# Giving three of 32 channel-block statistics to ScalarE in a GroupNorm, BatchNorm and binary 3x3 convolution kernel

## The chip, the cores and the metric

The kernel runs on one core of one Trainium2 chip. Its time is device time in microseconds (us), the median of three runs. The core's engines run side by side: TensorE (PE) multiplies matrices, VectorE (DVE) and ScalarE (ACT) work elementwise and reduce along rows, GpSimd (POOL) does elementwise work and issues transfers, SyncE (SP) issues transfers. They meet only at semaphores. SBUF is the on-chip memory with 128 partitions, PSUM holds matmul results.

## The reference

The input x is 16 images of 256 channels, 56 x 56 pixels, float32.

```python
g = GroupNorm(x)                 # 32 groups of 8 channels per image: mean and variance
mean, var = over (image, h, w) of g, per channel
xn = (g - mean) * rsqrt(var + 1e-4) * gamma + beta
t  = where(xn > 0, 1, -1)
xc = clip(xn, -1, 1)
y  = conv3x3(t, conv_w) + conv_b                 # 256 -> 256 channels
b  = (conv3x3(sum_c(xc * t), ones) + beta_b) / (conv3x3(sum_c |t|, ones) + beta_b)
out = x + y * b
```

The convolution of an image can't start until the scale and offset of each channel are known, and these need the mean and the variance of every channel of all 16 images. So the kernel reads all of x once for the statistics, and again for the convolution.

## The kernel before, in words

Channels lie on the partitions: 256 channels are two halves of 128. A *block* is one channel half of one image, 128 x 3136 float32, 1568 KB. There are 32 blocks.

**Statistics.** SP issues the load of each block in order (`stat_load`, L186). Four buffers of one block each take turns: the two halves of `y` and the two halves of `xb`, which the convolution uses later for other data. Load k waits until VectorE has read block k - 4 (L190), then goes out on SP's queue, which is in order: a load that waits holds up all behind it. The two weight loads (L202) go out after the first two blocks. For each block VectorE runs `statistics(k)` (L657): it waits for the load, takes seven `bn_stats` of 448 columns (L662), and after the second of them combines the seven results of the block before with one `bn_aggr` (L654) into that block's mean and variance in `mv`. The last `bn_stats` counts `stats_read` up, which frees the buffer. Between blocks 7 and 8, and between 11 and 12, VectorE does small work on the weights' scale (L682 to L699). The last two blocks, 30 and 31, are the two channel halves of image 0; they are loaded as halves of rows, 812 KB each, four loads in all (L205 to L208), in the layout in which the convolution reads them, and take eight `bn_stats` of 392 columns (L673). In the meantime GpSimd and ScalarE prepare the weights (L303 to L325, L351 to L374). ScalarE's last weight step is L374; then it waits for the statistics.

**Coefficients.** When `aggr_done` says that all 32 are there, PE averages the means and variances over the groups of eight channels by three small matmuls (L543 to L548), ScalarE takes square roots (L378, L381), and VectorE computes scale and offset per image and channel into `AB` (L724 to L753); `coef_ready` then lets all engines go on.

**Convolution.** For each image and each of four pieces g (channel half, row half) VectorE and ScalarE turn x into signs and into the transformed planes `V`, PE multiplies them with the transformed weights `U` (L570), ScalarE and VectorE take results out, and GpSimd's queue adds x and stores. A hardware loop goes over the images.

Of the kernel before, what the change touches and what calls it, by code (L numbers as in the profile page):

```python
# [9 lines left out]
ACT = mybir.ActivationFunctionType  # L10
AX = mybir.AxisListType

P = 128
NI, C, H, W = 16, 256, 56, 56
# [21 lines left out]
TERMS = tuple((ci, digits, dx) for ci in range(CT) for dx in (1, 0, 2) for digits in range(2))  # L36
PIECES = 7
PIECE = H * W // PIECES

LAST_PARTS = ((0, N // 2), (N // 2, N))  # L40


def conv_preact(nc, x, w_t, gamma, beta, conv_b, beta_b, consts, sum_rows, map_rows, out):
# [6 lines left out]
    with ExitStack() as ctx:  # L50
        def sb(name, shape, dt=F32):
            return ctx.enter_context(nc.sbuf_tensor(name, shape, dt))

        def sem(name):
            return ctx.enter_context(nc.semaphore(name))
# [29 lines left out]
        inv_8 = sb("inv_8", [P, CT])  # L85
        st = sb("st", [P, 2, CT, 8, 6])
        mark = sb("mark", [P, 2, CT])
        mv = sb("mv", [P, NI, CT, 2])
        AB = sb("AB", [P, NI, 2, CT])
        eps = sb("eps", [P, 2])  # L90
# [22 lines left out]
        s_in = [[sem(f"s_in{a}{c}") for c in range(CT)] for a in range(2)]  # L113
        y_out = [sem(f"y_out{g}") for g in range(G4)]
        last_out = [sem(f"last_out{k}") for k in range(2)]
        x_added = [sem(f"x_added{g}") for g in range(G4)]
        stats_read, aggr_done = sem("stats_read"), sem("aggr_done")
        w_abs, wall, wrow, wscale = sem("w_abs"), sem("wall"), sem("wrow"), sem("wscale")
        w_pool, w_act, scale_ready = sem("w_pool"), sem("w_act"), sem("scale_ready")
        step, dev_ready, grp = sem("step"), sem("dev_ready"), sem("grp")  # L120
# [27 lines left out]
        def at_least(eng, s, value):  # L148

            if not (isinstance(value, int) and value <= 0):  # L150
                eng.wait_ge(s, value)

        def stat_image(k):

            pair, at = divmod(k, 4)
            return NI - 2 - 2 * pair + (at < 2), int(at < 2), at % 2

        def stat_buffer(a, c):

            if a:  # L160
                return y[:, 2 * c:2 * c + 2].rearrange("p g f -> p (g f)")
            return xb[:, c].rearrange("p h f -> p (h f)")[:, 0:H * W]

        def own_rows(g):

            first = W * (g // 2)
            return xb[:, g % 2, g // 2, first:first + HPX]
# [16 lines left out]
        @block.sync  # L184
        def _(sp):
            def stat_load(k):  # L186

                m, a, c = stat_image(k)
                if k >= 4:
                    sp.wait_ge(stats_read, k - 3)  # L190
                sp.dma_start(stat_buffer(a, c), x_rows[m, c]).then_inc(s_in[a][c], 16)

            def load_rows(src, g):

                h = g // 2
                first = (HR - 1) * W * h
                sp.dma_start(xb[:, g % 2, h], src[g % 2, :, first:first + XR * W]).then_inc(x_in[g], 16)

            stat_load(0)
            stat_load(1)  # L200
            for c in range(CT):
                sp.dma_start(wt[:, c], w_v[:, c].rearrange("p (a b o) -> p a b o", a=3, b=3)).then_inc(w_in[c], 16)  # L202
            for k in range(2, 2 * NI - 2):
                stat_load(k)
            for c in range(CT):  # L205
                sp.wait_ge(stats_read, 2 * NI - 5 + c)
                for g in (c, 2 + c):
                    load_rows(x_rows[0], g)  # L208

            def crow_load(m):  # L210

                sp.wait_ge(cs8_ready, m + 1)
                sp.dma_start(sum_rows[m, W:W + H * W].rearrange("(k f) -> k f", f=SQ), cs98[:, :])\
                  .then_inc(cs_stored, 16)
                sp.wait_ge(cs_stored, 16 * m + 16)
                at_least(sp, vsum_ready, m)
                sp.dma_start(crow[:, :, 1:W + 1], row_windows[m].rearrange("r (k w) -> r k w", w=W))\
                  .then_inc(crow_in, 16)

            def load(n, src, g):  # L220

                sp.wait_ge(u_ready, 4 * n + g + 4)
                sp.wait_ge(abs_done, 4 * n + g + 5)
                load_rows(src, g)

            def first_load(g):

                if g:
                    sp.wait_ge(u_ready, g)
                else:  # L230
                    sp.wait_ge(u0_ready, 1)
                sp.wait_ge(abs_done, g + 1)
                load_rows(x_rows[1], g)

            def map_load(n, h):

                if h:
                    at_least(sp, scaled, 4 * n)
                sp.dma_start(bmap[:, h, :],
                             map_rows[n:n + 1, h * HPX:(h + 1) * HPX].to_broadcast([P, HPX]))\  # L240
                  .then_inc(bmap_in[h], 16)

            def map_store(n):

                sp.wait_ge(bm_ready, n + 1)
                sp.dma_start(map_rows[n].rearrange("(r w) -> r w", w=W), bm[:, :]).then_inc(bm_stored, 16)
                sp.wait_ge(bm_stored, 16 * n + 16)

            def image(n, ahead=None):

                crow_load(n)
                if ahead is not None:
                    load(n, ahead, 0)
                map_store(n)
                map_load(n, 0)
                if ahead is not None:
                    load(n, ahead, 1)
                map_load(n, 1)
                if ahead is not None:
                    load(n, ahead, 2)  # L260
                if ahead is not None:
                    load(n, ahead, 3)

            for g in range(G4):
                first_load(g)
            load(0, x_rows[2], 0)
            load(0, x_rows[2], 1)
            sp.wait_ge(zeros_in, 16)
            crow_load(0)
            map_store(0)  # L270
            map_load(0, 0)
            map_load(0, 1)
            load(0, x_rows[2], 2)
            load(0, x_rows[2], 3)
            for n in range(1, NI - 2):
                image(n, x_rows[n + 2])
            image(NI - 2)
            image(NI - 1)

            for k, (lo, hi) in enumerate(LAST_PARTS):  # L280
                sp.wait_ge(last_added, k + 1)
                sp.dma_start(out_v[NI - 1, 1, 1][:, 4 * lo:4 * hi], y[:, 3, 4 * lo:4 * hi]).then_inc(last_out[k], 16)
            for g in range(G4):

                sp.wait_ge(y_out[g], 16 * (NI - (g == 3)))
            for k in range(2):
                sp.wait_ge(last_out[k], 16)
# [54 lines left out]
        def _(act):  # L342
# [31 lines left out]
                    nc.scalar.activation(U[:, ci, 0, k], src, ACT.Copy).then_inc(w_act, 1)  # L374


            act.wait_ge(grp, 3)
            nc.scalar.activation(tmp[:, 3, :], acc[:, 0, 0, 0:NI * CT], ACT.Sqrt, bias=eps[:, 0:1])\  # L378
              .then_inc(root_out, 1)
# [145 lines left out]
        def _(pe):  # L525
# [13 lines left out]

            pe.wait_ge(cst_in, 16)  # L540
            grouped = cst[:, C_GROUP:C_GROUP + P]
            pe.wait_ge(aggr_done, 2 * NI)
            nc.tensor.matmul(csum[:, 0:NI * CT], grouped, mv[:, :, :, 0].rearrange("p n c -> p (n c)"),  # L543
                             start=True, stop=True).then_inc(grp, 1)
            nc.tensor.matmul(acc[:, 0, 0, 0:NI * CT], grouped, mv[:, :, :, 1].rearrange("p n c -> p (n c)"),
# [86 lines left out]
        def _(dve):  # L632
# [16 lines left out]
            def aggregate(k):  # L649

                m, a, c = stat_image(k)
                dve.wait_ge(stats_read, k + 1)
                nc.vector.memset(mark[:, a, c:c + 1], 0.0)
                nc.vector.bn_aggr(mv[:, m, c, :], st[:, a, c] if k >= 2 * NI - 2 else st[:, a, c, 0:PIECES])\  # L654
                  .then_inc(aggr_done, 1)

            def statistics(k):  # L657

                m, a, c = stat_image(k)
                dve.wait_ge(s_in[a][c], 16 * (k // 4) + 16)  # L660
                for j in range(PIECES):
                    ins = nc.vector.bn_stats(st[:, a, c, j], stat_buffer(a, c)[:, j * PIECE:(j + 1) * PIECE])  # L662
                    if j == 1 and k:
                        aggregate(k - 1)
                ins.then_inc(stats_read, 1)

            def last_statistics(c):

                k = 2 * NI - 2 + c
                for h in range(2):  # L670
                    dve.wait_ge(x_in[2 * h + c], 16)
                    for j in range(4):
                        ins = nc.vector.bn_stats(st[:, 0, c, 4 * h + j], own_rows(2 * h + c)[:, j * N:(j + 1) * N])  # L673
                        if h == 0 and j == 1:
                            aggregate(k - 1)
                ins.then_inc(stats_read, 1)

            for k in range(8):
                statistics(k)
# [18 lines left out]
                                          ALU.mult, ALU.add))  # L698
            chain(nc.vector.reciprocal(rcount[:, :], rcount[:, :]))  # L699
            for k in range(12, 2 * NI - 2):  # L700
                statistics(k)
            for c in range(CT):
                last_statistics(c)
            aggregate(2 * NI - 1)

            mean = mv[:, :, :, 0].rearrange("p n c -> p (n c)")
# [14 lines left out]
                chain(nc.vector.scalar_tensor_tensor(out=s, in0=t, scalar=1.5, in1=s,  # L721
                                                     op0=ALU.add, op1=ALU.mult))

            dve.wait_ge(aggr_done, 2 * NI)  # L724
            dve.wait_ge(grp, 1)
            chain(nc.vector.tensor_tensor(d, mean, csum[:, 0:NI * CT], ALU.subtract))
            nc.vector.tensor_tensor(d2, d, d, ALU.mult).then_inc(dev_ready, 1)
# [283 lines left out]
```

## Time and profile before

| what | value |
|---|---|
| median of three runs | 937.71 us (937.62 to 938.79) |
| time of the profiled execution | 937.77 us |
| its span, from the first to the last instruction | 936.0 us |
| PE busy | 782.9 us, 84% |
| VectorE busy | 790.4 us, 84% |
| ScalarE busy | 581.3 us, 62% |
| GpSimd busy | 140.8 us, 15% |

The span and the time of the same execution are 1.77 us apart. Busy shares are averages over two very different stages. Of the 40 slices that the page cuts the span into (23.4 us each), the first six show PE nearly idle and VectorE full, and the slices behind them show PE full. The granted clock of PE in the same slices is 0.5 from the second to the sixth and 0.9 or more (of 2.4 GHz) behind them.

### The profile page before, as it was taken

The numbers are of one execution on the slowest core, as the hardware profiler recorded it, in microseconds if no ns is written. First come the engines' busy times: TensorE is split into PE (matmuls) and PEld (weight loads), VectorE is DVE, ScalarE is ACT, GpSimd is POOL, SyncE is SP. The second block draws the span as 40 slices with busy tenths as digits, with TensorE's granted clock in tenths as the row PEclk, the third lists the DMA queues.
The fourth block names the chain that finished last, engine by engine and source line by source line (L and its number), as shares of the span: only waits on it lengthen the run. The fifth ranks groups of instructions, "written<-read, shape, count | busy, mean of one in ns | idle before, by whom it ended". The sixth has DMA issues, their size and how long they took to land. (4 is left out here: it accounts for less than half of the span.)

```text
span 936.0 us, 12745 instructions
## 1 busy us (share of the span) xinstructions
PE 782.9 (84%) x4686; PEld 464.9 (50%) x4686; DVE 790.4 (84%) x1244; ACT 581.3 (62%) x469; POOL 140.8 (15%) x160
## 2 busy tenths in 40 slices
PE   2100003999999999999999999999999999999996
PEld 2100002555555555555555555555555555555553
DVE  4999998989888888888797979787878797879755
ACT  2043105968777777777777777776868686868310
POOL 0089300001111111101111111111111111101011
PEclk9755555999999999999999999999999999999998
DMA  9999972468888887888797969696969696958589
GB/s 360 429 408 377 411 323 70 142 182 259 252 249 231 243 238 220 265 213 275 192 296 174 314 161 318 163 310 165 308 171 297 174 297 185 293 157 215 131 214 268
DMA packets 43478, 232.79 MB, mean 249 GB/s; under 512 B 10560, under 2 KB 10688, under 8 KB 39360
## 3 DMA queue, kind: packets, MB, share of 16 engines
q0 software_dynamic: 18144, 101.16, 41.8%
q1 hardware_dynamic: 24544, 131.25, 38.7%
q10 hardware_dynamic: 768, 0.12, 0.1%
q8 instruction: 9, 0.15, 0.1%
q14 instruction: 13, 0.11, 0.0%
HBM read 180.73 MB, written 51.79 MB: 248 GB/s over the span
## 5 line engine op out<-in xcount | busy, mean ns | idle before, releaser
L570 PE MATMUL acc<-V,U 128*128 128x385 f16 (+1 forms) x4608 | 769.4, 331 | 11.8 <-DVE V L790 10.1
L570 PEld LDWEIGHTS acc<-V,U 128*128 128x128 f16 x4608 | 450.9, 98 | 325.8 <-issue 12.7
L442 ACT ACTIVATE sn<-acc,inv_s 128x784 f32<-128x784 f32 x128 | 116.9, 913 | 207.1 <-PE acc L570 201.2
L335 POOL DMA_DIRECT2D y<-x x63 | 53.9, 856 | 728.7 <-DVE y L877 715.2
L877 DVE SCALAR_TENSOR_TENSOR y<-y,vec,bmap 128x1568 f32<-128x1568 f32 (+1 forms) x65 | 117.7, 1810 | 0.2
L420 ACT ACTIVATE r<-xb,ab 128x1568 f32<-128x1568 f32 x64 | 106.6, 1690 | 6.0 <-ACT u L395 4.0
L395 ACT ACTIVATE u<-xb,ab 128x1624 f16<-128x1624 f32 x63 | 109.0, 1732 | 0.2
L405 ACT ACTIVATE T<-u 128x1680 f16<-128x1680 f16 x60 | 95.6, 1594 | 2.0 <-DVE D L784 2.0
L408 ACT ACTIVATE T<-T 128x1568 f16<-128x1568 f16 x58 | 87.6, 1510 | 1.8
L543 PE MATMUL csum<-mv,cst 128*128 128x32 f32 x2 | 0.6, 396 | 94.9 <-DVE mv L654 94.9
L784 DVE TENSOR_TENSOR D<-T 128x1568 f16<-128x1568 f16 x63 | 61.4, 974 | 15.1 <-ACT T L408 14.3
L849 DVE SCALAR_TENSOR_TENSOR ds<-sn 128x784 f32<-128x784 f32 x64 | 62.0, 968 | 5.9 <-ACT sn L442 5.9
L662 DVE BATCH_NORM_STATS2 st<-y 128x6 f32<-128x448 f32 x112 | 60.2, 600 | 6.6 <-DMA y<-x 6.5
L819 DVE SCALAR_TENSOR_TENSOR ssum<-r 128x1568 f32<-128x1568 f32 x32 | 57.3, 1791 | 3.5 <-ACT r L426 2.0
L826 DVE TRANSPOSE_TENSOR_REDUCE quarter<-ssum 128x49 f32<-128x1568 f32 x32 | 57.8, 1805 | 0.1
L662 DVE BATCH_NORM_STATS2 st<-xb 128x6 f32<-128x448 f32 x98 | 52.6, 598 | 6.1 <-DMA xb<-x 6.1
L330 POOL DMA_DIRECT2D out<-y x63 | 51.7, 821 | 9.9 <-DMA y<-x 9.3
L777 DVE TENSOR_SCALAR T<-T 128x784 f16<-128x784 f16 x64 | 22.5, 351 | 32.8 <-ACT T L405 32.6
L426 ACT ACTIVATE r<-r 128x1568 f32<-128x1568 f32 x32 | 48.4, 1511 | 1.0
L865 DVE SCALAR_TENSOR_TENSOR y<-acc,inv_s,ds 128x392 f32<-128x392 f32 x64 | 39.7, 620 | 9.8 <-PE acc L570 9.8
L543 PEld LDWEIGHTS csum<-mv,cst 128*128 128x128 f32 x2 | 0.5, 313 | 94.9 <-issue 94.9
L854 DVE SCALAR_TENSOR_TENSOR y<-sn,ds 128x392 f32<-128x392 f32 x64 | 36.3, 568 | 9.3 <-DMA out<-y 2.7
(99 smaller groups left out, 396.2 us busy)
## 6 DMA issues: line engine op xcount, KB each, us to landing
xb<-x SPq DMA_DIRECT2D x64, 812.0 KB, 6.4
y<-x POOLq DMA_DIRECT2D x63, 784.0 KB, 7.7
out<-y POOLq DMA_DIRECT2D x63, 784.0 KB, 9.4
y<-x SPq DMA_DIRECT2D x16, 1568.0 KB, 8.3
bmap<-map_rows SPq DMA_DIRECT2D x32, 784.0 KB, 6.1
xb<-x SPq DMA_DIRECT2D x14, 1568.0 KB, 8.7
V<-w_t SPq DMA_DIRECT2D x2, 1152.0 KB, 14.6
out<-y SPq DMA_DIRECT2D x2, 392.0 KB, 2.8
```

The lines of the kernel that those rows point to most:

```text
L395: nc.scalar.activation(u[:, g % 2, 1:1 + XR], by_row(xb[:, c, g // 2]), ACT.Sign, scale=ab[:, a, 0, c:c + 1], bias=ab[:, a, 1, c:c + 1])\
L405: nc.scalar.activation(T[:, 30:60], u[:, g % 2, h:h + HR + 2], ACT.Relu, scale=2.0).then_inc(t_ready, 1)
L408: nc.scalar.activation(T8[:, :], T[:, 30:30 + HR], ACT.Copy, scale=4.0, bias=-3.0)\
L420: nc.scalar.activation(r[:, c, 0:HPX], own_rows(g), ACT.Abs, scale=ab[:, a, 0, c:c + 1], bias=ab[:, a, 1, c:c + 1]).then_inc(abs_done, 1)
L442: nc.scalar.activation(sn[:, b, half], acc[:, b, :, 0:N], ACT.Copy, scale=inv_s[:, b:b + 1])\
L570: last = nc.tensor.matmul(by_row(acc[:, g % 2, bank, 0:N])[:, :, lo:hi], U[:, ci, digits, k, dx, co * P:(co + 1) * P], by_row(V[:, a, ci, ...
L662: ins = nc.vector.bn_stats(st[:, a, c, j], stat_buffer(a, c)[:, j * PIECE:(j + 1) * PIECE])
L784: nc.vector.tensor_tensor(d[:, 0], T[:, 32:32 + HR], T8[:, :], ALU.subtract).then_inc(cq_done, 1)
L819: nc.vector.scalar_tensor_tensor(out=ssum[:, :], in0=r[:, 0, 0:HPX], scalar=1.0, in1=r[:, 1, 0:HPX], op0=ALU.min, op1=ALU.subtract).then_i ...
L826: nc.vector.tensor_reduce(quarter[:, h, :], ssum[:, :].rearrange("p (b i) -> p b i", i=SQ), AX.X, ALU.add, apply_transpose=True).then_inc( ...
L849: nc.vector.scalar_tensor_tensor(out=ds[:, :, :], in0=sn[:, b, 0], scalar=2.0, in1=sn[:, b, 1], op0=ALU.mult, op1=ALU.subtract).then_inc(d ...
L877: nc.vector.scalar_tensor_tensor(out=y[:, g, lo:hi], in0=y[:, g, lo:hi], scalar=vec[:, 2, b:b + 1], in1=bmap[:, h, lo:hi], op0=ALU.add, op ...
```

## The change

ScalarE takes the statistics of blocks 21, 24 and 27 (`ACT_BLOCKS`). For each it waits for the load and runs five instructions: a Copy of the block onto itself whose accumulator gives the sum of each row; the sum times 1/3136, written as the mean; the sum times -1/3136; a Square of the block with that as bias, onto itself, whose accumulator gives the sum of squares about the mean; and that sum times 1/3136, written as the variance. Between dependent ones ScalarE waits on its own semaphore. The Square frees the buffer (`act_read`).

VectorE leaves these blocks out, with their `bn_aggr`. SP's waits for a free buffer go to `act_read` for these three blocks and to a recounted `stats_read` for the others. PE and VectorE wait for `act_var` beside `aggr_done` before they use the statistics.

```diff
+ACT_BLOCKS = (21, 24, 27)
+        sums = sb("sums", [P, len(ACT_BLOCKS), 3])
+        act_sum, act_mean, act_read, act_var = (sem(s) for s in ("act_sum", "act_mean", "act_read", "act_var"))
+        def vector_count(k):
+            return k + 1 - sum(b <= k for b in ACT_BLOCKS)
+        def block_read(eng, k):
+            if k in ACT_BLOCKS:
+                eng.wait_ge(act_read, ACT_BLOCKS.index(k) + 1)
+            else:
+                eng.wait_ge(stats_read, vector_count(k))
@@ SP, stat_load and the loads of image 0
                 if k >= 4:
-                    sp.wait_ge(stats_read, k - 3)
+                    block_read(sp, k - 4)
             for c in range(CT):
-                sp.wait_ge(stats_read, 2 * NI - 5 + c)
+                block_read(sp, 2 * NI - 6 + c)
@@ ScalarE, behind the weights and ahead of act.wait_ge(grp, 3)
+            def statistics(j, k):
+                m, a, c = stat_image(k)
+                act.wait_ge(s_in[a][c], 16 * (k // 4) + 16)
+                nc.scalar.activation(stat_buffer(a, c), stat_buffer(a, c), ACT.Copy, accum_out=sums[:, j, 0:1])\
+                  .then_inc(act_sum, 1)
+                act.wait_ge(act_sum, j + 1)
+                nc.scalar.activation(mv[:, m, c, 0:1], sums[:, j, 0:1], ACT.Copy, scale=1.0 / (H * W))
+                nc.scalar.activation(sums[:, j, 1:2], sums[:, j, 0:1], ACT.Copy, scale=-1.0 / (H * W))\
+                  .then_inc(act_mean, 1)
+                act.wait_ge(act_mean, j + 1)
+                nc.scalar.activation(stat_buffer(a, c), stat_buffer(a, c), ACT.Square, bias=sums[:, j, 1:2],
+                                     accum_out=sums[:, j, 2:3]).then_inc(act_read, 1)
+                act.wait_ge(act_read, j + 1)
+                nc.scalar.activation(mv[:, m, c, 1:2], sums[:, j, 2:3], ACT.Copy, scale=1.0 / (H * W))\
+                  .then_inc(act_var, 1)
+            for j, k in enumerate(ACT_BLOCKS):
+                statistics(j, k)
@@ PE and VectorE, ahead of the coefficients
-            pe.wait_ge(aggr_done, 2 * NI)
+            pe.wait_ge(act_var, len(ACT_BLOCKS))
+            pe.wait_ge(aggr_done, 2 * NI - len(ACT_BLOCKS))
-            dve.wait_ge(aggr_done, 2 * NI)
+            dve.wait_ge(act_var, len(ACT_BLOCKS))
+            dve.wait_ge(aggr_done, 2 * NI - len(ACT_BLOCKS))
@@ VectorE: aggregate waits for the recounted stats_read and takes the last block that is VectorE's own
-                dve.wait_ge(stats_read, k + 1)
+                dve.wait_ge(stats_read, vector_count(k))
-                        aggregate(k - 1)
+                        aggregate(previous(k))
             for k in range(12, 2 * NI - 2):
-                statistics(k)
+                if k not in ACT_BLOCKS:
+                    statistics(k)
```

## Rows read from the trace of the kernel before

**Rows 1.** Busy time by stage: window, its length, engines' busy us (instructions), PEclk, DMA, GB/s.

```profile
70.00:80.00 10.00, 0.00 (x0) 0.00 (x0) 10.00 (x25) 0.00 (x0) 10.00 (x7) 0.50 0.88 321
20.00:50.00 30.00, 8.98 (x35) 7.36 (x33) 28.01 (x65) 0.00 (x0) 1.44 (x1) 0.71 1.01 430
80.00:96.00 16.00, 0.00 (x0) 0.00 (x0) 16.00 (x38) 9.47 (x13) 14.68 (x9) 0.50 1.00 421
112.00:126.00 14.00, 0.00 (x0) 0.00 (x0) 14.00 (x34) 0.00 (x0) 0.00 (x0) 0.50 0.99 411
400.00:600.00 200.00, 200.00 (x1211) 118.28 (x1210) 167.35 (x236) 147.30 (x118) 22.59 (x32) 1.00 0.83 236
```

**Rows 2.** Who waited for whom, PE: us in total, times, longest.

```profile
PE csum L543 <- DVE mv L654: 94.9, 1, 94.9
PE acc L570 <- DVE V L790: 10.1, 1, 10.1
```

**Rows 3.** VectorE in order of time: start, us, instructions merged, idle before.

```profile
21.86 1.15 DVE L662 BATCH_NORM_STATS2 st<-xb 128x6 f32<-128x448 f32 x2 [6.08 <-DMA xb<-x]
96.81 1.13 DVE L662 BATCH_NORM_STATS2 st<-y 128x6 f32<-128x448 f32 x2
104.61 1.13 DVE L662 BATCH_NORM_STATS2 st<-xb 128x6 f32<-128x448 f32 x2
...
128.03 1.12 DVE L662 BATCH_NORM_STATS2 st<-y 128x6 f32<-128x448 f32 x2
135.82 1.01 DVE L673 BATCH_NORM_STATS2 st<-xb 128x6 f32<-128x392 f32 x2
141.01 2.84 DVE L673 BATCH_NORM_STATS2 st<-xb 128x6 f32<-128x392 f32 x6
145.12 0.19 DVE L726 TENSOR_TENSOR ssum<-mv,csum 128x32 f32<-128x32 f32 x1 [0.86 <-PE csum L543]
```

**Rows 4.** SP's issues in order of time: start, from first to last, line.

```profile
93.02 4.23 SPq L191 DMA_DIRECT2D xb<-x  x2
100.82 4.23 SPq L191 DMA_DIRECT2D y<-x  x2
116.42 4.23 SPq L191 DMA_DIRECT2D y<-x  x2
128.12 0.81 SPq L197 DMA_DIRECT2D xb<-x  x2
```

**Rows 5.** Single loads, KB, us to landing: blocks 22; 21, 25; 24; 28; 29; last two.

```profile
xb<-x SPq DMA_DIRECT2D x1, 1568.0 KB, 8.1
y<-x SPq DMA_DIRECT2D x1, 1568.0 KB, 8.2
y<-x SPq DMA_DIRECT2D x1, 1568.0 KB, 8.0
y<-x SPq DMA_DIRECT2D x1, 1568.0 KB, 7.7
y<-x SPq DMA_DIRECT2D x1, 1568.0 KB, 8.5
xb<-x SPq DMA_DIRECT2D x2, 812.0 KB, 7.4
```

**Rows 6.** ScalarE: groups by line and form up to 160 us, and its last weight step.

```profile
L353 ACT ACTIVATE V<-V 128x2304 f32<-128x2304 f32 x2 | 4.2, 2122 | 10.0 <-DMA V<-w_t 10.0
L362 ACT ACTIVATE V<-V 128x768 f32<-128x768 f32 x2 | 1.7, 842 | 45.3 <-POOL V L308 45.3
L420 ACT ACTIVATE r<-xb,ab 128x1568 f32<-128x1568 f32 x2 | 3.3, 1680 | 0.0
L426 ACT ACTIVATE r<-r 128x1568 f32<-128x1568 f32 x1 | 1.5, 1511 | 0.0
L387 ACT ACTIVATE ab<-AB 128x4 f32<-128x4 f32 x1 | 0.2, 205 | 1.8 <-DVE AB L753 1.8
...
96.41 1.28 ACT L378 ACT_TABLE_LOAD   x1
```

**Rows 7.** PE's first products, and its clock around them (columns as in rows 1).

```profile
156.00:160.00 4.00, 3.65 (x14) 1.82 (x15) 3.93 (x9) 3.97 (x4) 0.00 (x0) 0.60 0.53 159
160.00:164.00 4.00, 4.00 (x26) 2.35 (x24) 3.96 (x6) 3.18 (x3) 0.00 (x0) 1.00 0.74 253
```

More of the change, by code:

```diff
@@ L655, in aggregate, with previous @@
                   .then_inc(aggr_done, 1)
+            def previous(k):
+                return max(b for b in range(k) if b not in ACT_BLOCKS)
             def statistics(k):
@@ L674, in last_statistics @@
                         if h == 0 and j == 1:
-                            aggregate(k - 1)
+                            aggregate(previous(k))
                 ins.then_inc(stats_read, 1)
```

## The prediction

> **What bounds the kernel now.** I read the busy time by stage first. From 200 us on PE is busy without a gap (200.00 of 200 us in one such window) at its full clock [rows 1]; nothing that is done before can change that stretch except by letting it begin earlier. Then PE's waits: it sat idle for 94.9 us until the last `bn_aggr`, and for 10.1 us from the coefficients to the first `V` planes [rows 2]. So a microsecond taken off the statistics stage is a microsecond off the kernel. Who sets the pace of that stage? VectorE has been busy without a gap since 21.86 us, when it last waited for a load [rows 3], and it is full in each window of rows 1 behind that. Blocks 20 and 21 take it from 96.81 to 104.61 us [rows 3], 3.90 us a block. But the loads are close behind it: they move 411 to 430 GB/s with a DMA share of 0.99 to 1.01 [rows 1], and 411 GB/s is 1.606 MB (1568 KB) every 3.90 us, VectorE's own pace. The reader is to see two things near a balance: VectorE is the bound, and the transfers have little speed in hand.
>
> How much they have is the heart of the sum, so I work out landings from issue and time to landing. Load 22 goes out at 93.02 and takes 8.1 us [rows 4, 5], so it lands at 101.1; VectorE turns to block 22 at 104.61 [rows 3]: a lead of 3.5 us. Load 28 lands at 116.42 + 7.7 = 124.1, used at 128.03: lead 3.9. Load 29 goes out at 116.42 + 4.23 - 0.33 = 120.32 and lands 8.5 later, at 128.8; it is used at 128.03 + 3.90 = 131.93: lead 3.1. The last two half loads land 7.4 us after 128.12 and 128.6, so the last is there by about 136.8 (their single times may lie some tenths on either side of the median); its half of block 31 is read from about 142.0, by the last four of the six `bn_stats` between 141.01 and 143.85 [rows 3].
>
> **VectorE, what is removed.** Three blocks, each seven `bn_stats`, one `bn_aggr` and one memset: 3 x 3.90 = 11.7 us of VectorE's work. If the loads could follow, the whole 11.7 us would come off.
>
> **The loads, what is late next.** They can't follow. When VectorE leaves out block 21 it stands before block 22 at 96.81 + 3.90 = 100.71 us, and that block lands at 101.1. The first block left out is worth 104.61 - 101.1 = 3.5 us, and the lead is then used up. From there each block is read when it lands. The other two blocks left out take load off an engine that already waits; they give nothing but slack.
> What decides the end is then how fast blocks 22 to 31 land. Lower end of the gain: the landings stay where they are. The read of block 29 starts at 128.8 instead of 131.93, and behind it come 3.90 us for block 29 and the two last blocks as before, so the end moves by 3.1 us (block 28 alone would allow 3.9, and the last half load 142.0 - 136.8 = 5.2). Upper end: the loads keep the 430 GB/s that they reached between 20 and 50 us with more loads queued [rows 1], 3.73 us a block. Then block 29 lands at 101.1 + 7 x 3.73 = 127.2, used 4.7 us earlier than before, and block 28 at 123.5, 4.5 us earlier: gain 4.5 us. Between them: blocks 22 to 28 landed (124.1 - 101.1) / 6 = 3.83 us apart, while in a window with 421 GB/s it is 3.81 us. Loads will now be issued up to 3.5 us earlier, so more of them queue and the stream should not be slower than that. At 3.81 block 29 lands at 127.8 and block 28 at 124.0, gains of 4.1 and 4.0. I take 3.8 us, between this and the unchanged landings, because load 29's late landing (8.5 us against 7.7) looks like a single hiccup that may or may not be there again.
>
> **ScalarE, what is added.** Per block, a Copy over 3136 columns. From 768 columns in 842 ns and 2304 in 2122 ns it is 0.833 ns a column [rows 6], so 2.82 us. The Square has a bias from SBUF: with two such operands 1568 columns took 1680 ns against 1511 ns with none [rows 6], so 2.8 to 3.0 us. Three one-column Copies at 0.2 us each [rows 6], two of them ahead of the Square. The accumulator output is in no row; the nearest rows bound it between nothing and another 0.2 us instruction each, and an extra one is likely since a sum has to be written after the last column. With the waits between dependent instructions I take 6.7 us from landing to free buffer (6.1 to 7.3).
> ScalarE is free at 96.41 us, when its last weight step ends [rows 6], and block 21 lands at 89.12 + 8.2 = 97.3 (its load goes out 3.90 us ahead of load 22). Freed at 104.0. VectorE freed it before load 25, which went out at 104.72 [rows 4]. So although ScalarE takes 1.7 times as long, it starts 3.4 us sooner, on landing, and load 25 goes out no later. Likewise block 24 lands at 100.82 + 8.0 = 108.8 [rows 4, 5], is freed at 115.5, and load 28 went out at 116.42. Block 27 lands at about 120.3, is freed at 127.0, and the two half loads behind it went out at 128.12 [rows 4]. The other loads go out 3.5 us sooner with VectorE. SP's queue is in order, so a late `act_read` would hold all of these; by this sum each comes 0.7 to 1.1 us ahead of where it stands now.
> ScalarE's own queue: behind the three blocks stand only the square root of the coefficients, needed after 140 us, and its table load of 1.28 us [rows 6], which moves from 96.41 to about 127 and stays hidden. If Square needed a table of its own, block 21 would be freed 1.3 us later, at 105.3; load 25 had 8.2 us to landing against the 3.73 us that its bytes need, so it sat in a queue, and 0.6 us of delay vanish there.
>
> **What is added to other engines.** One more wait each on PE and VectorE ahead of the coefficients, on an event that is some 11 us old by then: nothing. VectorE's `bn_stats` next to a ScalarE that reads and writes SBUF: from 80 to 96 us ScalarE was busy 9.47 us and GpSimd 14.68, VectorE's pace was the same 3.90, so nothing.
>
> **Sum.** 936.0 - 3.8 = 932.2 us of span, 937.77 - 3.8 = 933.97 for the profiled execution, which lies 0.06 above the median of the runs. Forecast: 933.9 us.
>
> A rule of the Trainium skill speaks against the change. DMA: Bandwidth & Descriptors (Specifications) gives a limit of about 358 GB/s for HBM per core beside a fabric ceiling of 435 GB/s. By the first, an estimate from that page, a block takes 4.49 us, the loads would be the bound already and the change would bring nothing. The trace disagrees for this core alone on its HBM, with 430 GB/s over 30 us [rows 1]; it stands close to the page's second figure, by which a block can't come in under 3.69 us.
>
> **Rivals.**
> *The stream slows in its last third (little or no gain).* Before, 3.1 to 3.9 us of lead hide a slow spell; after, none does, and it goes to the end. Such a spell is in the trace: 321 GB/s from 70 to 80 us [rows 1], though part of it is VectorE's own pause for the weights' scale, and VectorE did not wait. If a spell of that depth (5.00 us a block) hit three blocks behind 22, they would cost 3 x 1.2 = 3.6 us, the gain would be near 0.2 us, and the time 937.5. A milder one (one block and a half) gives 936. Against it: from 80 us on no window is under 411 GB/s, which is demand.
> *The loads are the bound already (no gain).* Then blocks 0 to 31 would come in at the loads' pace with and without ScalarE's help, 937.7 us. Against it: VectorE waits for no load after 21.86 us [rows 3], and 430 GB/s is 4% more than its pace needs. This is what the page's lower limit would make of it.
> *The loads are faster than ever seen (more gain).* VectorE would need a block every 3.0 us to give the full 11.7 us, 926.0 us in all. That is 535 GB/s, and the highest in rows 1 is 430. A gain a little over 4.7 is all that I leave room for.
> *PE's clock comes back later (slower).* PE stands at 0.5 of its clock, 1.2 GHz, through the wait, starts its products at 156.35, and is granted 2.4 GHz within 160 us [rows 7]. The start moves by 3.8 us, and the grant might not move with it. Each us at the lower level costs half a us of product time. To eat the gain it must last 7.6 us longer than the 3 or so now; to be over 0.2% slower (another 1.9 us), 11.4 us longer, giving 939.6 us. For it speaks only that the rule of the grant isn't visible in the rows; against it that full PE work was followed by the grant at once.
> *ScalarE is late (less gain).* If it took 10 us a block instead of 6.7, load 28 would go out at 118.8 and land by 126.5, block 28 would be read only 1.5 us earlier than before: 936.2 us. It decides from about 7.3 us a block: load 28 takes 7.7 us where little is queued ahead of it [rows 5], and to land at 124.0 it must be out by 116.3 at the least, and block 24 lands at 108.8; up to there the queue ahead hides it.
>
> **Chances.** Forecast, a gain between 2.6 and 4.7 us: 0.80. Slow stream 0.08, loads the bound already 0.01, ScalarE late 0.04, faster than 4.7 us 0.04, clock 0.03. A measurement of this kernel tells 0.2%, 1.9 us, from no change. Faster by over that: 0.80 + 0.04, and some 0.03 of the milder forms of the slow stream and of ScalarE: 0.87. Within: 0.10. Slower: 0.03. The range reaches from 4.9 us of gain (the upper end and 0.4 for a PE clock that returns sooner) to 1.8: 932.8 to 935.9.
>
> **What would show it.** VectorE idle ahead of block 22 for 0.4 us or so, and in all about 11.7 - 3.8 = 7.9 us idle between 100 and 140 us, all put down to DMA; the first coefficient step (L726) at 141.3 instead of 145.12; time to landing of 10 us or more for loads 26 to 29, since they are issued earlier into the same stream; loads 25, 28 and the last two issued by ScalarE's `act_read` at 104.0, 115.5 and 127.0; ScalarE's two long instructions near 2.8 and 2.9 us; PE's 200 us windows unchanged. It would be wrong if VectorE did not wait at all (then the loads have more in hand), if GB/s fell under 400 between 100 and 130 us, or if SP sat waiting for ScalarE while the transfers ran dry.

## The result

The changed kernel takes 934.9 us, the median of ten runs (933.24 to 938.35), against 938.11 us (937.28 to 941.72) for the kernel before in the same comparison: a ratio of 0.996, 95% interval 0.9948 to 0.9972. The profiled execution took 934.54 us with a span of 932.7 us, where the kernel before had 937.77 and 936.0. Forecast were 933.9 us and a gain of 3.8 us; measured is a gain of 3.2 us by the medians and 3.3 us by the spans. The kernel before had come out at 938.11 us here instead of the 937.71 that the forecast started from, so 0.4 of the 1.0 us by which the time is over the forecast has nothing to do with the change.

In the busy time by stage (columns as in [rows 1], where the window from 112 to 126 us stands at 411 GB/s) VectorE is no longer full, while the loads go faster. PE's later windows are what they were.

```profile
112.00:126.00 14.00, 0.00 (x0) 0.00 (x0) 9.76 (x24) 9.06 (x11) 0.00 (x0) 0.50 1.01 428
152.00:156.00 4.00, 3.47 (x13) 1.71 (x14) 3.93 (x8) 3.97 (x3) 0.00 (x0) 0.58 0.47 138
156.00:160.00 4.00, 4.00 (x26) 2.36 (x25) 3.96 (x6) 3.19 (x4) 0.00 (x0) 1.00 0.78 265
400.00:600.00 200.00, 200.00 (x1212) 118.31 (x1209) 167.41 (x235) 147.41 (x117) 23.70 (x34) 1.00 0.81 236
```

VectorE in order of time, after the change; in brackets its idle time and what ended it. These answer to [rows 3].

```profile
97.10 1.14 DVE L702 BATCH_NORM_STATS2 st<-y 128x6 f32<-128x448 f32 x2
...
101.50 1.15 DVE L702 BATCH_NORM_STATS2 st<-xb 128x6 f32<-128x448 f32 x2 [0.41 <-DMA xb<-x]
...
112.90 1.15 DVE L702 BATCH_NORM_STATS2 st<-y 128x6 f32<-128x448 f32 x2 [3.49 <-DMA y<-x]
...
124.14 1.15 DVE L702 BATCH_NORM_STATS2 st<-y 128x6 f32<-128x448 f32 x2 [3.34 <-DMA y<-x]
...
131.96 1.02 DVE L713 BATCH_NORM_STATS2 st<-xb 128x6 f32<-128x392 f32 x2
...
141.29 0.19 DVE L768 TENSOR_TENSOR ssum<-mv,csum 128x32 f32<-128x32 f32 x1 [0.89 <-PE csum L579]
```

Block 22 starts at 101.50, block 25 at 112.90 and block 28 at 124.14, each as its load lands, after 0.41, 3.49 and 3.34 us of idle time: 7.2 us that VectorE gained and didn't use. The *first coefficient step* is VectorE's first instruction behind the statistics (L726 before, L768 after); it tells when the stage is done, and the experiments are compared by it. It comes at 141.29 instead of 145.12, 3.83 us sooner.

SP's issues in order of time, after, which answer to [rows 4]: the loads of blocks 25, 26, 28 and 29 and the last two half loads.

```profile
104.06 0.33 SPq L206 DMA_DIRECT2D y<-x  x1
105.53 0.33 SPq L206 DMA_DIRECT2D xb<-x  x1
...
115.45 0.33 SPq L206 DMA_DIRECT2D y<-x  x1
116.92 0.33 SPq L206 DMA_DIRECT2D y<-x  x1
...
126.73 0.80 SPq L212 DMA_DIRECT2D xb<-x  x2
```

The time to landing of three of them, blocks 26, 28 and 29, which answers to [rows 5] (that of block 27 was 11.0 us):

```profile
xb<-x SPq DMA_DIRECT2D x1, 1568.0 KB, 11.1
...
y<-x SPq DMA_DIRECT2D x1, 1568.0 KB, 8.7
...
y<-x SPq DMA_DIRECT2D x1, 1568.0 KB, 10.9
```

Loads 26 and 29, issued 3.1 and 3.4 us sooner than before, wait in a longer queue; load 28, which hangs on ScalarE, goes out only 1.0 us sooner (115.45 against 116.42) and has the shortest queue ahead of it.

And ScalarE's first block, which answers to [rows 6]:

```profile
97.76 2.82 ACT L396 ACTIVATE y<-y 128x3136 f32<-128x3136 f32 x1 [1.08 <-DMA y<-x]
100.49 0.19 ACT L396 ACTIVATION_READ_ACCUMULATOR y<-y 128x1 f32 x1
...
101.03 2.91 ACT L403 ACTIVATE y<-y,sums 128x3136 f32<-128x3136 f32 x1
103.85 0.19 ACT L403 ACTIVATION_READ_ACCUMULATOR y<-y,sums 128x1 f32 x1
```

Each accumulator costs one more instruction of 0.19 us. The buffer is free at 104.04, 6.3 us after ScalarE began, and load 25 goes out at 104.06.

### The profile page after: what moved, and what is told of

The parts are those of the page before. It is cut to its first block and busy times, and to the rows that moved or that the text cites. A ratio compares the mean times of both kernels' runs of the same rounds, so it can differ in the third digit from the quotient of the medians.

```text
span 932.7 us, 12739 instructions
## 1 busy us (share of the span) xinstructions
PE 782.7 (84%) x4686; PEld 464.9 (50%) x4686; DVE 779.0 (84%) x1217; ACT 600.6 (64%) x490; POOL 141.4 (15%) x160
## 5 line engine op out<-in xcount | busy, mean ns | idle before, releaser
L702 DVE BATCH_NORM_STATS2 st<-y 128x6 f32<-128x448 f32 x98 | 52.9, 606 | 13.4 <-DMA y<-x 13.3
L702 DVE BATCH_NORM_STATS2 st<-xb 128x6 f32<-128x448 f32 x91 | 49.0, 606 | 6.8 <-DMA xb<-x 6.8
L461 ACT ACTIVATE r<-r 128x1568 f32<-128x1568 f32 x32 | 48.4, 1511 | 1.0
```

## The experiments

The theory (A) is that of the prediction: VectorE was one block ahead of the loads' arrival and no more; one block left out uses that up, and then the loads set the pace. Its rivals: each block taken from VectorE gives its share (B); or ScalarE holds its buffers so long that SP's in-order queue starves the transfers, and that ate the rest (C).

**Block 21 alone, and block 27 alone.**

```diff
-ACT_BLOCKS = (21, 24, 27)
+ACT_BLOCKS = (21,)      # in the other kernel (27,)
```

> ScalarE takes block 21 alone; VectorE takes 24 and 27 again. Theory A (the loads set the pace once the lead of some 3.5 us is used up; one block left out uses it up): as fast as the changed kernel within 0.5 us, some 3.5 us under the kernel before; VectorE waits once, ahead of block 22, and the first coefficient step starts near 141.4 us. Theory B (each block taken from VectorE gives its share, a third of 3.8 us): 1.3 us under the kernel before, first coefficient step at 143.8. Theory C (ScalarE frees its buffers late, SP's in-order queue holds the loads, and that ate the other 8 us): faster than the changed kernel, since only one buffer is held.

> ScalarE takes block 27 alone. Theory A: VectorE is 3.9 us early at block 28 and waits there for its load; leads of 3.1 to 3.9 us at blocks 28 and 29 give a gain of 3.1 to 3.9 us over the kernel before, first coefficient step 141.2 to 142.0, about 0.4 us later than with block 21 since no load goes out earlier than before. Theory B: 1.3 us gain, as for block 21.

Block 21 alone: 935.5 us, ratio to the kernel before 0.9968 (0.9954 to 0.9983). Block 27 alone: 935.47 us, 0.9972 (0.9956 to 0.9987). The first coefficient step, in the order of time of VectorE, first of the kernel with 21 and then of that with 27:

```profile
141.60 0.19 DVE L768 TENSOR_TENSOR ssum<-mv,csum 128x32 f32<-128x32 f32 x1 [0.89 <-PE csum L579]
```

```profile
124.44 1.15 DVE L702 BATCH_NORM_STATS2 st<-y 128x6 f32<-128x448 f32 x2 [0.39 <-DMA y<-x]
...
141.59 0.19 DVE L768 TENSOR_TENSOR ssum<-mv,csum 128x32 f32<-128x32 f32 x1 [0.89 <-PE csum L579]
```

One block gives 3.5 us of the 3.8, whichever it is; B, which wanted 143.8, falls. C wanted the kernel with one held buffer to be faster than the changed one, and it isn't. Three details were off. With block 21 alone VectorE did not wait at block 22 at all in that execution: load 22 went out at 93.28 us and took 7.7 us, so it landed at 101.0, just as VectorE stood before it. The lead was used up to the last tenth, and nothing was over to wait for. The 0.4 us between the two kernels didn't show. And by the medians the gains are 2.8 and 2.9 us, not the 3.5 that the first coefficient step gives; where the rest goes is told below, with what was mis-sized.

**The loads made light.** In the changed kernel and in the kernel before:

```diff
-                sp.dma_start(stat_buffer(a, c), x_rows[m, c]).then_inc(s_in[a][c], 16)
+                n = H * W if k < 4 else H * W // 2
+                sp.dma_start(stat_buffer(a, c)[:, 0:n], x_rows[m, c][:, 0:n]).then_inc(s_in[a][c], 16)
```

> The changed kernel, but the loads of blocks 4 to 29 bring only the first half of each row (the second half of the buffer keeps what was there), so the transfers carry half the bytes there while VectorE and ScalarE do all their work. Theory A: with the loads out of the way VectorE's whole 11.7 us come off against the kernel before: first coefficient step near 133.4, time 11 to 12 us under the kernel before. Theory C (ScalarE's late release is what limits): the gain stays near that of the changed kernel, 4 to 6 us.

> The kernel before, with the loads of blocks 4 to 29 cut to the first half of each row as in the changed kernel's run. If VectorE sets the pace of the statistics in the kernel before: no gain, first coefficient step at 145 us as in the kernel before, 938 us, within 0.5 us. If the loads had a share in the pace: 1 us or more is gained.

The changed kernel with half loads: 928.31 us, ratio to the kernel before 0.989 (0.9872 to 0.9909). The kernel before with half loads: 938.29 us, 0.9988 (0.9972 to 1.0003). VectorE's first coefficient step in the one and in the other:

```profile
133.97 0.19 DVE L769 TENSOR_TENSOR ssum<-mv,csum 128x32 f32<-128x32 f32 x1 [0.89 <-PE csum L580]
```

```profile
145.17 0.19 DVE L727 TENSOR_TENSOR ssum<-mv,csum 128x32 f32<-128x32 f32 x1 [0.86 <-PE csum L544]
```

This pair settles what held back the other 8 us. In the kernel before the loads had no share in the pace: 145.17 against 145.12 us. In the changed kernel, with ScalarE and its held buffers as they are, half the bytes free 7.3 us more, 11.2 us in all of the 11.7 us that VectorE gave away. What held them back was bytes on the way, not ScalarE. The time itself missed its forecast of 11 to 12 us: it is 10.0 us under the kernel before by the medians, so over 1 us of the 11.2 is lost behind the coefficients.

**ScalarE made late.**

```diff
+                nc.scalar.activation(stat_buffer(a, c), stat_buffer(a, c), ACT.Copy).then_inc(act_extra, 1)
+                act.wait_ge(act_extra, j + 1)
                 nc.scalar.activation(stat_buffer(a, c), stat_buffer(a, c), ACT.Copy, accum_out=sums[:, j, 0:1])\
                   ...
```

> The changed kernel with one more Copy of the whole block onto itself ahead of each of ScalarE's three, some 2.8 us more per block, so it frees its buffers 9.2 us after landing instead of 6.4. Prediction's sum (it decides from 7.3 us): load 28 goes out near 118.2 instead of 115.5 and lands near 125.9; block 28 starts 1.7 to 2.2 us later than in the changed kernel, and so does the first coefficient step: 143.0 to 143.5, time some 2 us over the changed kernel. If ScalarE's time doesn't matter: no change against the changed kernel.

937.11 us, ratio to the kernel before 0.9982 (0.997 to 0.9994). Load 28 goes out at 118.22, block 28 starts at 126.41, and the first coefficient step is at 143.55, 2.3 us later than in the changed kernel; by the medians the kernel is 2.2 us slower than the changed one (937.11 against 934.9). VectorE and SP in order of time:

```profile
114.26 1.15 DVE L704 BATCH_NORM_STATS2 st<-y 128x6 f32<-128x448 f32 x2 [5.00 <-DMA y<-x]
...
118.22 0.80 SPq L206 DMA_DIRECT2D y<-x  x2
...
126.41 1.15 DVE L704 BATCH_NORM_STATS2 st<-y 128x6 f32<-128x448 f32 x2 [4.24 <-DMA y<-x]
...
143.55 0.19 DVE L770 TENSOR_TENSOR ssum<-mv,csum 128x32 f32<-128x32 f32 x1 [0.89 <-PE csum L581]
```

So mechanism C is real, but begins beyond what ScalarE takes: 2.85 us more per block cost 2.3 us at the end, which leaves 0.6 us of slack, near the 0.9 us that the prediction had between ScalarE's 6.4 and its bound of 7.3 us.

**A block taken early.** If the loads are the bound from the moment that the lead is gone, more is to be had only where the loads themselves lose time. In the kernel before they moved 321 GB/s from 70 to 80 us [rows 1]. ScalarE is idle before its weight steps, so it can take block 7:

```diff
-ACT_BLOCKS = (21, 24, 27)
+ACT_BLOCKS = (7, 21, 24, 27)   # in others (7, 15, 21, 24, 27), (7,) and (7, 21, 29)
@@ ScalarE, ahead of its weight steps
+            for j, k in enumerate(ACT_BLOCKS):
+                if k < 12:
+                    statistics(j, k)
@@ ScalarE, between the two halves of its weight steps
+                if ci == 1 and 15 in ACT_BLOCKS:
+                    statistics(ACT_BLOCKS.index(15), 15)
@@ ScalarE, behind its weight steps
             for j, k in enumerate(ACT_BLOCKS):
-                statistics(j, k)
+                if k > 15:
+                    statistics(j, k)
@@ VectorE (the same for blocks 8 to 11)
             for k in range(8):
-                statistics(k)
+                if k not in ACT_BLOCKS:
+                    statistics(k)
```

> The changed kernel, and ScalarE also takes block 7, ahead of its weight steps. VectorE is 3.9 us earlier from 45 us on, and so are the issues of the loads behind. If the slow spell of the loads (60 to 80 us, some 360 GB/s) is only demand, the gain adds: first coefficient step 137.5 to 138.5, time 3 to 4 us under the changed kernel. If the loads are slow there by themselves, VectorE meets them at blocks 13 to 18 and waits; landings from block 18 on stay where they are, and the gain over the changed kernel is under 1 us.

> As before, and ScalarE takes block 15 too, between its two halves of weight steps. By the theory that the loads bound all from the moment the lead is used up: no more than 0.5 us under the kernel with block 7, or later if ScalarE's weight steps, some 6.4 us later behind block 15, push block 21 back. By the theory that VectorE's load counts: another 1.3 to 3.9 us off.

> The changed kernel again, unaltered, on the same chip as the two with earlier blocks: 3.0 to 3.8 us under the kernel before, first coefficient step at 141.0 to 141.7.

With block 7: 931.13 us, 0.991 (0.9886 to 0.9934), first coefficient step at 137.44. With 7 and 15: 931.27 us, 0.991 (0.9887 to 0.9934), at 137.82. The changed kernel beside them: 935.03 us, 0.9958 (0.9943 to 0.9973), at 140.87. Block 7 gives another 3.9 us by the medians and 3.4 us at the first coefficient step. Two steps came 0.1 us ahead of the ranges that were forecast for them (137.44 and 140.87, against 137.5 and 141.0). The window from 60 to 80 us shows where, first in the changed kernel, then with block 7:

```profile
60.00:80.00 20.00, 0.00 (x0) 0.00 (x0) 19.90 (x48) 7.29 (x10) 18.91 (x12) 0.50 0.94 356
```

```profile
60.00:80.00 20.00, 0.00 (x0) 0.00 (x0) 19.90 (x49) 6.82 (x9) 18.76 (x12) 0.50 1.00 428
...
80.00:96.00 16.00, 0.00 (x0) 0.00 (x0) 16.00 (x38) 9.45 (x11) 14.91 (x10) 0.50 1.01 430
```

and VectorE in order of time with block 7 taken, at blocks 22, 25, 28 and 30:

```profile
97.87 1.15 DVE L708 BATCH_NORM_STATS2 st<-xb 128x6 f32<-128x448 f32 x2 [1.16 <-DMA xb<-x]
...
109.06 1.16 DVE L708 BATCH_NORM_STATS2 st<-y 128x6 f32<-128x448 f32 x2 [3.29 <-DMA y<-x]
...
120.29 1.15 DVE L708 BATCH_NORM_STATS2 st<-y 128x6 f32<-128x448 f32 x2 [3.33 <-DMA y<-x]
...
128.11 1.02 DVE L719 BATCH_NORM_STATS2 st<-xb 128x6 f32<-128x392 f32 x2
```

The loads now run at 424 to 435 GB/s in each window from 20 to 126 us, and the slow spell is gone: it was not a property of those transfers or of that time. A fifth block then gives nothing, as expected of a stage in which VectorE waits for loads from block 22 on, with and without it.

**Which blocks are worth it.** These rows show one more place. With block 7 on ScalarE, blocks 24 and 27 buy only 3.3 us of idle time each, while at the end VectorE still does blocks 29, 30 and 31 one behind the other.

> ScalarE takes blocks 7, 21 and 29; VectorE takes 24 and 27 again. With block 7 on ScalarE the loads run at 3.73 us a block to the end and VectorE waits 3.3 us each at blocks 25 and 28, so taking 24 and 27 back costs nothing. What ends the stage there is VectorE's own tail: blocks 29, 30 and 31 one behind the other, 4.5 us behind the last landing. Without 29 the tail ends 1.9 us behind the last half load: first coefficient step 135.3 to 136 us against 137.4, time 1.5 to 2.1 us under the kernel with blocks 7, 21, 24 and 27. If the loads' end were the bound there already: no gain.

> ScalarE takes block 7 alone. VectorE is one block, 3.90 us, ahead from 45 us on and needs 3.90 us for each of the others, more than the 3.73 us of a load, so it never waits for a load behind block 8 and the stage ends one block earlier: first coefficient step near 141.2, time 3.4 to 3.9 us under the kernel before, as with block 21 alone; GB/s from 60 to 80 us above 400. If loads that start early bring more by themselves: under 141.

> The kernel with blocks 7, 21, 24 and 27 again, unaltered, beside the one with 7, 21 and 29 on the same chip: 7.0 to 8.0 us under the kernel before, first coefficient step near 137.5.

Blocks 7, 21 and 29: 929.22 us, 0.991 (0.989 to 0.9931), first coefficient step at 135.37. Blocks 7, 21, 24 and 27 again: 931.02 us, 0.9923 (0.9906 to 0.9939), at 137.49. Block 7 alone: 934.81 us, 0.9955 (0.9937 to 0.9972), at 141.18. VectorE with 7, 21 and 29:

```profile
97.88 1.15 DVE L708 BATCH_NORM_STATS2 st<-xb 128x6 f32<-128x448 f32 x2 [1.01 <-DMA xb<-x]
...
126.01 1.04 DVE L719 BATCH_NORM_STATS2 st<-xb 128x6 f32<-128x392 f32 x2 [0.72 <-DMA xb<-x]
...
135.37 0.19 DVE L776 TENSOR_TENSOR ssum<-mv,csum 128x32 f32<-128x32 f32 x1 [0.89 <-PE csum L585]
```

Three blocks, as many as in the change, but chosen by where VectorE is late: the stage ends 9.75 us before that of the kernel before (145.12), against 3.83 us in the change, and the whole is some 9 us shorter by the medians (929.22 against 938.27). Block 7 alone shows the other half: 141.18, one block of 3.9 us, because from there VectorE at 3.90 us a block never caught up with loads that can land every 3.73 us.

## Why the prediction was right, point by point

*What bounds.* PE can only be moved, VectorE sets the pace of the statistics: right. Half loads left the kernel before at 145.17 us.

*The lead of 3.1 to 3.9 us as the size of the gain.* Right, and the heart of it: 3.83 us at the first coefficient step, forecast 3.8. Block 21 or block 27 alone gives 3.5. The two others gave 0.3 us more and otherwise idle time, 7.2 us against 7.9 forecast. The block that decided was 28, read on landing 3.89 us sooner than before; load 29 landed at 127.8, where the prediction had it, 0.2 us before VectorE stood before it, so the hiccup of load 29 that the 3.8 us allowed for did not come.

*The loads with more of them queued.* Right for the stream: loads 26, 27 and 29 took 11.1, 11.0 and 10.9 us to landing, over the 10 that the prediction named for loads 26 to 29. Load 28, with 8.7 us, did not: it waits for ScalarE's buffer and goes out late. Blocks 22 to 28 landed 3.77 us apart (3.81 forecast), and from 112 to 126 us the rate was 428 GB/s, near its upper bound of 430.

*ScalarE.* 2.82 and 2.91 us for the long instructions (2.82 and 2.8 to 3.0 forecast). Loads 25, 28 and the last two went out at 104.06, 115.45 and 126.73, where 104.0, 115.5 and 127.0 stood. The first of these is closer than the sum deserves: from landing to free buffer it took 6.3 us, not 6.7, and block 21 landed at 97.7, not 97.3, and the two errors cancel. The bound of about 7.3 us is borne out by the late ScalarE to within a few tenths.

*The limit of about 358 GB/s* of the Trainium skill, DMA: Bandwidth & Descriptors (Specifications), would have made the gain nothing. Its row works the figure out as half of the 716 GB/s of an HBM stack that two cores share, and this kernel runs on one core, so it was no bound here. With block 7 on ScalarE the loads held 428 to 430 GB/s in windows of 20 and 16 us. That page's fabric ceiling of 435 GB/s is the figure that these rows stay under.

*PE's clock.* Right for the profiled pair, by luck in part. Products start at 152.53 instead of 156.35, and the granted clock is full in the window from 156 us instead of from 160 [rows 7]: PE ran its first products at 1.2 GHz for 2.8 us before and for 2.9 us after. But a second trace of the same changed kernel, and one of the kernel with a late ScalarE, show the grant coming later. First the two windows of the changed kernel again, then one of the late ScalarE:

```profile
152.00:156.00 4.00, 3.89 (x13) 1.77 (x14) 3.93 (x8) 3.97 (x4) 0.00 (x0) 0.50 0.59 182
156.00:160.00 4.00, 4.00 (x25) 2.34 (x24) 3.97 (x5) 2.99 (x3) 0.00 (x0) 0.97 0.70 234
```

```profile
156.00:160.00 4.00, 4.00 (x14) 1.79 (x13) 3.97 (x9) 3.96 (x3) 0.00 (x0) 0.50 0.91 258
```

In the first, products start at 152.11 and the full clock comes at about 156.3, 4.2 us later. In the second they start at 154.79 and the full clock comes at 160.0, 5.2 us later; 14 products fit into 4 us at 1.2 GHz where 26 fit at 2.4 GHz. So the prediction's rival that the grant need not move with the start is real, though small: each us at the lower level costs half a us, as the prediction had it. What decides when the grant comes isn't visible in these rows.

*What was mis-sized.* The sum took the gain at the coefficients as the gain at the end. Of 3.83 us 3.2 to 3.3 arrived. Two things lie between them. One is PE's clock, as told. The other is in the waits from 160 to 220 us, first before, then after:

```profile
DVE vsum L832 <- DMA crow<-sum_rows: 2.4, 1, 2.4
...
PE csum L555 <- DVE quarter L826: 0.2, 1, 0.2
```

```profile
DVE vsum L874 <- DMA crow<-sum_rows: 2.8, 1, 2.8
...
PE csum L591 <- DVE quarter L868: 0.7, 1, 0.7
```

In the first image the channel sums go to HBM and come back, VectorE waits for them, and PE waits for what VectorE does next. SP issued the store at 182.92 and the load at 189.53 before, 6.6 us apart, and 179.12 and 186.16 after, 7.0 us. PE's wait is 0.5 us longer, which is the whole loss of the profiled pair. In the changed kernel run again VectorE's wait there is 1.5 us and PE has none, so the round trip differs from one execution to the next of the same kernel and is not an effect of the change. Both together, all times in us:

| kernel | first coefficient step | products at 1.2 GHz for | PE's wait for `quarter` | from first coefficient step to end of span |
|---|---|---|---|---|
| before | 145.12 | 2.8 | 0.2 | 790.9 |
| changed | 141.29 | 2.9 | 0.7 | 791.4 |
| changed, again | 140.87 | 4.2 | none | 791.4 |
| block 21 alone | 141.60 | 4.7 | 0.5 | 792.0 |
| late ScalarE | 143.55 | 5.2 | 0.9 | 793.2 |
| changed, half loads | 133.97 | 4.2 | 0.4 | 792.3 |
| 7, 21, 24 and 27, again | 137.49 | 3.5 | none | 790.6 |
| 7, 21 and 29 | 135.37 | 3.8 | 0.4 | 792.1 |

The last column differs by up to 2.6 us. Take off half of the time at 1.2 GHz and PE's wait, and it is 788.9 to 789.8 in all of them. So the first coefficient step tells what the statistics gained, and what follows takes up to 2.3 us more than in the kernel before, by an amount that differs from one execution to the next. That fits block 21 alone, with 3.5 us at the step and 2.8 by the medians, and half loads, with 11.2 and 10.0; of the other executions behind the medians there is no trace.

*What it left out.* The rival "no more than 430 GB/s, so little beyond 4.7 us" was right for these three blocks and wrong as a bound on the idea: the loads lost time from 60 to 80 us, hidden in the kernel before by the lead, and the prediction read that spell as a danger, not as 3.4 us to be had at the first coefficient step.

*In part open.* Why the loads ran at 356 GB/s from 60 to 80 us. In that window the changed kernel and the one with block 7 alone each issued five loads, with medians of 8.8 to 8.9 and 8.6 to 8.8 us to landing, and yet the one moved 356 and the other 429 GB/s. But what lands there was issued from 52 us on, and there the two differ. VectorE's work on the weights' scale (45.3 to 48.4 us) holds up the read of block 8 in the kernel before, so load 12 goes out at 52.40, 7.0 us behind load 11. With block 7 alone it goes out at 48.67, 1.5 us behind. SP's issues of loads 12 and 13 and the time to landing of load 13, first before, then with block 7 alone:

```profile
52.40 4.23 SPq L191 DMA_DIRECT2D y<-x  x2
...
y<-x SPq DMA_DIRECT2D x1, 1568.0 KB, 8.2
```

```profile
48.67 4.23 SPq L206 DMA_DIRECT2D y<-x  x2
...
y<-x SPq DMA_DIRECT2D x1, 1568.0 KB, 10.7
```

In the kernel before, loads 13 and 16 go out 3.2 and 3.0 us ahead of the landing of the load in front of them, and land 5.0 and 5.3 us behind it; with block 7 alone load 13 goes out 7.0 us ahead and lands 3.7 us behind. Load 12 itself doesn't fit: it goes out 3.4 us ahead in the kernel before and lands 3.7 us behind. So the spell goes with loads that join the stream late, and VectorE's two pauses (the other is from 64.0 to 65.6 us) make loads 12 and 16 late. GpSimd's work is not the cause: it is busy 18.91 and 18.76 of the 20 us in the two kernels. None of the runs took the pauses away alone, and why a late load lands that far behind isn't shown.

## What to carry to other kernels

When work is taken off the busiest engine of a streaming stage whose transfers move nearly as fast as it reads, the gain is not the work's duration but the lead of the transfers over that engine: landing time (issue plus time to landing) against the start of use, the smallest over the blocks that follow. Work taken off beyond that lead becomes idle time, so choose the pieces by place: one early, before the stream first loses its queue, and one at the tail, where the last pieces are done one behind the other. A slower engine can take a block at no cost if it starts on landing, as long as the buffer comes free before the queue of loads ahead of its next load has run short: holding it for 6.3 us cost nothing that shows here, and 2.85 us more cost 2.3. Judge such a change first by the step at which the stage ends, since what follows can differ by more than the change is worth.

## What the hardware showed

The accumulator output of a ScalarE instruction adds an instruction of its own, ACTIVATION_READ_ACCUMULATOR, of 0.19 us; the pass over 3136 columns takes 2.82 us with it as it does without (in the kernel with a late ScalarE both stand side by side). Copy, Square and the accumulator needed no table load beyond those of the kernel before; the one of 1.28 us ahead of the square root moved from 96.41 to 126.96 us and stayed hidden. PE ran its first products at 1.2 GHz for 2.8 us in the kernel before and for 2.9 to 5.2 us in the kernels of the table above that start them sooner, with a different time in two executions of the same kernel. The transfers into SBUF held 430 GB/s beside a VectorE, a ScalarE and a GpSimd that were all busy (16.00, 9.45 and 14.91 of 16 us).
